# Second attention layer, edge stage: running sums kept in two PSUM accumulator banks and copied out by ScalarE at each item

## The reference

```
q, k, v = h @ W_qkv + b_qkv                      # 8 heads of 32
score   = sum_d(q[dst] * k[src]) * SCALE         # per edge and head
ex      = exp(score - max over the edges of dst)
attn    = ex / (sum of ex over the edges of dst)
h_new   = segment_sum(attn * v[src], dst) @ W_out + b_out
```

## Time and profile before

| what | value |
|---|---|
| median of 3 runs | 2125.84 us (2121.98 to 2130.7) |
| profiled execution, first to last instruction | 2134.3 us |
| whole span: TensorE busy | 1761.5 us |
| VectorE busy | 1539.6 us |
| GpSimd busy | 1160.5 us |
| ScalarE busy | 1070.3 us |
| edge stage of the second layer, first gather to last sum | 1243.6 to 1899.9 us |

### The profile page before, as it was taken

One profiled execution on the slowest core, in us unless ns is written; L12 is line 12 of the kernel. 1 busy time (PEld: TensorE's weight loads), 2 busy tenths in 40 slices (PEclk: granted clock), 3 DMA queues, 4 the chain that ended last, 5 costly groups with the idle time before them and its releaser, 6 DMA issues. The chain is left out here.

```text
span 2134.3 us, 41549 instructions
## 1 busy us (share of the span) xinstructions
PE 1761.5 (83%) x10388; PEld 1537.1 (72%) x10389; DVE 1539.6 (72%) x2788; ACT 1070.3 (50%) x2353; POOL 1160.5 (54%) x1169
## 2 busy tenths in 40 slices
PE   3699999999999989828973868888888888866278
PEld 3499999999999979728972756666666766645267
DVE  5388888888888845643545849899999898847622
ACT  1677777777777726403420145445455454316133
POOL 0376666666666601462443457777777777512112
PEclk7799999999999989758996989999999999867579
DMA  3443333333333312133323566666666666524310
GB/s 96 133 121 111 104 108 108 104 107 108 105 106 108 98 31 80 69 124 98 119 75 98 193 185 189 189 188 188 193 191 186 190 187 188 148 65 141 115 38 29
DMA packets 132538, 267.55 MB, mean 125 GB/s; under 512 B 24030, under 2 KB 75888, under 8 KB 132407
## 3 DMA queue, kind: packets, MB, share of 16 engines
q0 software_dynamic: 63456, 191.61, 30.7%
q1 hardware_dynamic: 68534, 73.21, 11.2%
q10 hardware_dynamic: 416, 1.18, 0.2%
HBM read 225.34 MB, written 42.50 MB: 125 GB/s over the span
## 5 line engine op out<-in xcount | busy, mean ns | idle before, releaser
L319 POOL DMA_INDIRECT e_rows<-h_table,e_idx x440 | 453.4, 1030 | 214.1 <-issue 106.3
L1740 POOL DMA_INDIRECT a_rows<-kv_table,a_idx x440 | 476.1, 1082 | 135.8 <-issue 128.9
L619 PE MATMUL e_w<-w2h,e_hidl 128*128 128x256 f32 x880 | 247.7, 304 | 2.9 <-DVE e_msg L704 2.9
L589 PE MATMUL e_agg<-e_msg,e_hot 128*128 128x256 f32 x880 | 246.1, 402 | 0.0
L1822 PE MATMUL a_q<-q,a_spread 128*128 x880 | 233.7, 407 | 6.5 <-ACT a_spread L1782 6.3
L620 PE MATMUL e_w<-w2l,e_hidh 128*128 128x256 f32 x880 | 226.4, 280 | 0.0
L1853 PE MATMUL a_agg<-a_rows,x 128*128 128x264 f32 x880 | 226.2, 402 | 0.0
L704 DVE TENSOR_TENSOR e_msg<-e_w,e_rows 128x1024 f32<-128x1024 f32 x110 | 134.7, 1224 | 93.4 <-PE e_w L623 93.4
L1775 ACT ACTIVATE a_apart<-iota_n,dst_rel 128x128 f32<-128x128 f32 x440 | 140.6, 391 | 112.9 <-PE a_agg L1853 112.8
L1822 PEld LDWEIGHTS a_q<-q,a_spread 128*128 128x128 f32 x880 | 166.2, 199 | 38.9 <-issue 12.8
L1853 PEld LDWEIGHTS a_agg<-a_rows,x 128*128 128x128 f32 x880 | 168.2, 200 | 24.7
(11 more groups left out here) (456 smaller groups left out, 4221.4 us busy)
## 6 DMA issues: line engine op xcount, KB each, us to landing
e_ea<-in_eaT SPq DMA_DIRECT2D x220, 64.0 KB
m_rows<-expert_rows SPq DMA_DIRECT2D x32, 272.0 KB, 2.7
e_rows<-h_table,e_idx POOLq DMA_INDIRECT x440
a_rows<-kv_table,a_idx POOLq DMA_INDIRECT x440, 3.7
q_ab<-expert_out SPq DMA_DIRECT2D x50, 128.0 KB, 3.3
kv_table<-q_kv SPq DMA_DIRECT2D x25, 256.0 KB, 2.2
u_stage<-in_m_w SPq DMA_DIRECT2D x16, 256.0 KB
x<-in_x SPq DMA_DIRECT2D x1, 3200.0 KB, 13.9
```

The costliest lines, as they stand in the source:

```text
L319: c.nc.gpsimd.indirect_dma_start(out=rows[:, g.slot8, j, :], out_offset=None, in_=table, in_offset=bass.IndirectOffsetOnAxis(ap=idx[:, g.s ...
L589: last = mm(bank(wins[j]), hot[:, g.slot4, t, :], msg[:, g.slot4, t, :], start=False, stop=False, skip_group_check=True)
L619: mm(w, hidl[:, g.slot, cols[k]], w2h[:, k, :], start=(k == 0), stop=False)
L1740: nc.gpsimd.indirect_dma_start(out=rows[:, g.slot * IG + j, 0:2 * D], out_offset=None, in_=c.kv_dram, in_offset=bass.IndirectOffsetOnAxis( ...
```

## The change

- The sums no longer go through SBUF for every group. Two banks hold the running sums of the current window and the one before or after it, chosen by the window's parity. `add_item` on TensorE opens the *other* bank with a two-column matmul of zeros and adds one item to its own bank. ScalarE's `keep` copies the bank over the window's place in `c.sums` after each item. TensorE waits for that copy before the next item.
- The sums are one step later: group i-7 in step i (`SUM = LAG + 1`). The first item stands between the two halves of the q matmuls of step i (after both in place 3 of a chunk), the second at the end of the step.
- In ScalarE's queue the first copy heads the step, the second follows the spread copy.
- VectorE's per-group addition is gone. The rescaling moves to the bank, one step later (place 3), and reads a ScalarE copy of the factor (`grown`).
- The one-hot ring grows from 10 to 12 groups. The memset of the sums in `project_qkv` is gone; the edge stage starts with a small memset and two ScalarE copies that clear the banks.

```diff
@@ project_qkv, GpSimd
-                nc.gpsimd.memset(c.sums[:, :, :], 0.0).then_inc(s_clr, 1)
-                pool.wait_ge(s_clr, 1)
@@ attention_edges
+    SUM = LAG + 1
+    HR = 12
...
+        bank = lambda w: ap[:, bass.ds(w & 1, 1), 0:DM].rearrange("p a d -> p (a d)")
+        other = lambda w: ap[:, bass.ds((w + 1) & 1, 1), 0:DM].rearrange("p a d -> p (a d)")
@@ GpSimd
+                nc.gpsimd.memset(zero[:, :], 0.0).then_inc(s_zero, 1)
-                        need(pool, c.sem("poolgate"), (s_idx, g.n + 1), (s_agg, g.n - R + 1))
+                        need(pool, c.sem("poolgate"), (s_idx, g.n + 1), (s_agg, (g.n - R + 1) * JG))
@@ ScalarE
+                act.wait_ge(s_zero, 1)
+                for p in range(2):
+                    nc.scalar.copy(ap[:, p, 0:DM], zero[:, :]).then_inc(s_zero, 1)
+                def keep(a, j, wins):
+                    need(act, s_ag, (s_agg, a.n * JG + j + 1))
+                    nc.scalar.copy(window(c.sums, wins[j]), bank(wins[j])).then_inc(s_acc, 1)
                 def step(at):
                     i = at(0)
+                    a = at(-SUM)
+                    if real(a):
+                        wins = item_windows(act, c, a.n)
+                        keep(a, 0, wins)
...
-                        need(act, s_ag, (s_agg, g.n - R + 1), (s_hot, g.n))
+                        need(act, s_ag, (s_agg, (g.n - HR + 1) * JG), (s_hot, g.n))
...
                         nc.scalar.copy(spread[:, h.pair, :, :].rearrange("p a n -> p (a n)"), hT[:, :]).then_inc(s_sp, 1)
+                    if i.place == 2 and closed(i.chunk - 1):
+                        need(act, s_ag, (s_gr, i.chunk), (s_rs, 2 * (i.chunk - 1)))
+                        nc.scalar.copy(grown[:, :], grow).then_inc(s_gn, 1)
+                    if real(a):
+                        keep(a, 1, wins)
@@ TensorE
+                def add_item(m, j, both):
+                    own = (both + j) >> 1
+                    need(pe, None, (s_msg, m.n + 1), (s_acc, m.n * JG + j), *([(s_rs, 2 * m.chunk + 2)] if m.place == 0 and j == 0 else []), own=True)
+                    mm(other(own)[:, 0:2], none[:, :], none[:, 0:2], start=True, stop=False, skip_group_check=True)
+                    for half in range(CT):
+                        t = j * CT + half
+                        last = mm(bank(own), hot[:, hots(m, t), :], rows[:, m.slot * IG + t, D:ROW], start=False, stop=False, skip_group_check=True)
+                    last.then_inc(s_agg, 1)
...
                         for j in range(IG):
+                            if j == CT and real(m) and not late:
+                                add_item(m, 0, sums)
...
                             last = mm(qp[g.pair][:, j * D:(j + 1) * D], spread[:, g.pair, j, :], window(c.q, wins[j // CT]), start=True, stop=True)
                         last.then_inc(s_q, 1)
+                        if real(m) and late:
+                            add_item(m, 0, sums)
...
                     if real(m):
-                        need(pe, None, (s_msg, m.n + 1), (s_acc, m.n), own=True)
-                        mm(ap[:, 1, 0:DM], none[:, 0:P], none[:, 0:DM], start=True, stop=False, skip_group_check=True)
-                        for j in range(JG):
-                            ...
+                        add_item(m, 1, sums)
@@ VectorE
-                    a = at(-LAG - 1)
-                    if real(a):
-                        w = ahead.take(i.step, "sums", a.n)
-                        need(dve, s_dg, (s_agg, a.n + 1), (s_acc, a.n), *([(s_rs, 2 * a.chunk + 2)] if a.place == 0 else []))
-                        to = c.sums[:, bass.ds(w, JG), :]
-                        v.tensor_tensor(to, to, ap[:, :, 0:DM], ALU.add).then_inc(s_acc, 1)
+                    if i.place == 3 and closed(ch):
+                        w = ahead.take(i.step, "crossing", ch * (CH // IG))
+                        need(dve, s_dg, (s_gn, ch + 1), (s_acc, (i.n - SUM) * JG))
+                        to = bank(w)[:, 0:D].rearrange("p (h d) -> p h d", h=H)
+                        v.scalar_tensor_tensor(to, grown[:, :].rearrange("p (h a) -> p h a", a=1).broadcast_to([P, H, DH]), 1.0, to, ALU.add, ALU.mult).then_inc(s_rs, 1)
...
```

More of the change, by code:

```diff
@@ L1776, in step @@
                         need(act, s_ag, (s_ap, (g.n + 1) * IG))
-                        nc.scalar.activation(hot[:, four(g), :], apart[:, :, :], ACT.Relu, bias=1.0, scale=-1.0).then_inc(s_hot, 1)
+                        nc.scalar.activation(hot[:, hots(g, 0):hots(g, IG), :], apart[:, :, :], ACT.Relu, bias=1.0, scale=-1.0).then_inc(s_hot, 1)
                     h = at(2)
@@ L1811, in step @@
                         mm(carries[:, 0:2 * (CH + 1)], c.heads_of_row[:, :], c.carried[:, :, :].rearrange("p a t -> p (a t)"), start=True, stop=True).then_inc(s_ca, 1)
+                    m = at(-SUM)
+                    sums = ahead.take(i.step, "sums", m.n) if real(m) else None
+                    late = i.place == 3
                     g = at(1)
+                    if real(m) and not real(g):
+                        add_item(m, 0, sums)
                     if real(g):
@@ L1826, in step @@
                         tr(exs, exT[:, :], c.ident[:, :]).then_inc(s_xT, 1)
-                    m = at(-LAG)
-                    if real(m):
-                        moved = ahead.take(i.step, "sums", m.n) & 1
                     if real(at(2)):
                         ahead.fetch(i.then, "q", at(2).n)
-                    if real(at(1 - LAG)):
-                        ahead.fetch(i.then, "sums", at(1 - LAG).n)
+                    if real(at(1 - SUM)):
+                        ahead.fetch(i.then, "sums", at(1 - SUM).n)
                     h = at(2)
@@ L1838, in step @@
                         for j in range(IG):
-                            last = tr(hT[:, j * P:(j + 1) * P], hot[:, h.slot * IG + j, :], c.ident[:, :])
+                            last = tr(hT[:, j * P:(j + 1) * P], hot[:, hots(h, j), :], c.ident[:, :])
                         last.then_inc(s_ht, 1)
@@ L1845, in step @@
                     if real(m):
-                        need(pe, None, (s_msg, m.n + 1), (s_acc, m.n), own=True)
-                        mm(ap[:, 1, 0:DM], none[:, 0:P], none[:, 0:DM], start=True, stop=False, skip_group_check=True)
-                        for j in range(JG):
-                            to = ap[:, 0, 0:DM] if j == 0 else ap[:, bass.ds(moved, 1), 0:DM].rearrange("p a d -> p (a d)")
-                            for half in range(CT):
-                                t = m.slot * IG + j * CT + half
-                                last = mm(to, hot[:, t, :], rows[:, t, D:ROW], start=(j == 0 and half == 0), stop=False, skip_group_check=True)
-                        last.then_inc(s_agg, 1)
+                        add_item(m, 1, sums)
                     if i.place == 0 and closed(ch):
@@ L1859, in _ @@
                 pe.wait_ge(s_none, 1)
+                pe.wait_ge(s_zero, 3)
                 rounds(pe, step, 4, LAG + 1, Edges)
@@ L1896, in step @@
                         v.tensor_tensor(by_head(rows[:, four(m), D:2 * D]), by_head(rows[:, four(m), D:2 * D]), ex, ALU.mult).then_inc(s_msg, 1)
-                        ahead.fetch(i.then, "sums", m.n)
-                    if i.place == 2 and closed(ch):
-                        w = ahead.take(i.step, "crossing", ch * (CH // IG))
-                        need(dve, s_dg, (s_gr, ch + 1), (s_acc, i.n - LAG))
-                        to = c.agg[:, bass.ds(w, 1), 0:D].rearrange("p a (h d) -> p (a h) d", h=H)
-                        v.scalar_tensor_tensor(to, grow.rearrange("p (h a) -> p h a", a=1).broadcast_to([P, H, DH]), 1.0, to, ALU.add, ALU.mult).then_inc(s_rs, 1)
-                        to = flat(c.agg[:, bass.ds(w, 1), D:DM])
-                        v.scalar_tensor_tensor(to, grow, 1.0, to, ALU.add, ALU.mult).then_inc(s_rs, 1)
                     if real(i):
```

24 lines of the change are left out of this document (16 added, 8 removed).

## The result

The changed kernel takes 2192.01 us (median of 4 runs, 2186.57 to 2194.59), the kernel before 2126.73 beside it (4 runs, 2121.98 to 2130.7). The ratio is 1.0304, 95% interval 1.0284 to 1.0323. The forecast was 2156 with a range to 2182: the slower direction and the circle of waits came true, the size did not, +65 us for +30.

What follows compares the result with a forecast made beforehand. GpSimd's unbroken gathers, 5.59 us a group, bound the kernel before; the change closes a longer circle of waits. + 33 - 6 + 0.6 + 2 = + 30 us, 2134.3 to 2164 profiled, 2156 us as median; 8-in-10 range 2120 to 2182.

Steps and rivals of the forecast that it cites:

- The removed addition is worth nothing: Edge stage: dropping VectorE's additions, 76.7 us in all, gives GpSimd nothing back; its 5.59 us a group stays.
- rival 2: Edge stage: GpSimd's long gathers go too, a group could fall to 5.0 us; 2062 us, or 2092 for half; chance 0.08.
- A plain step of 5.57: Edge stage: one full circle of copy, one-hots, spread, half of q and first item takes 5.57 us.
- Place 1's carries, + 0.2: Place 1 of a four-step chunk: the carries matmul stands ahead of q and waits for scans, + 0.2 us.
- Places 2 and 3, + 1.18: Per chunk: first item behind all q matmuls + 0.92, exponentials' copy ahead of spread + 0.16, rescaling + 0.1 us.
- it just fits; I take + 0.1: Place 3: VectorE's rescaling, 4.2 us, is done before the first item by TensorE's route, 4.5; + 0.1 us (0 to 0.5).
- the steps' + 33: Edge stage: about 25 chunks at 23.66 us against 22.36 now, + 33 us; bounds + 13 and + 56.
- The memset, - 6: End of the projection: without GpSimd's memset, VectorE's stalled normalisation comes back, - 6 us (-4.7 to -6.2).
- the start, + 0.6: Start of the edge stage: two clearing copies stand ahead of the first row numbers, + 0.6 us.
- The end, + 2: End of the edge stage: about seven rounds of 6.0 us against six of 6.31, + 2 us (-8 to + 6).
- 1: Edge stage: the circle is shorter than GpSimd's period, GpSimd stays the bound, only the ends change; 2122 us; chance 0.12.
- 3: Edge stage: TensorE's clock falls; with a quarter of the steps so, + 45 us on top, 2200 us; chance 0.10.

Runs made afterwards that it cites:

- e4: Kernel before with VectorE's msg (v times ex) cut from 1024 to 32 columns: 2059.81 us, ratio 0.9696 to before.
- e3: Kernel before with VectorE's addition into the sums cut from 264 to 8 columns an item: 2103.37 us, ratio 0.9891 to before.
- f2: Changed kernel with TensorE's tails matmul ahead of the second item instead of behind it: 2177.39 us, ratio 1.0229 to before.
- g3: Changed kernel with VectorE's product ahead of msg in place 2 alone: 2179.01 us, ratio 1.0244 to before.
- e1: Changed kernel with GpSimd's memset of the sums put back at the projection's end: 2198.89 us, ratio 1.0339 to before.
- f3: Changed kernel with two unread fill matmuls behind each item of the last eight steps: 2178.79 us, ratio 1.0242 to before.
- f1: Changed kernel with ScalarE's one-hots moved from ahead of the spread copy to the step's end: 2183.72 us, ratio 1.0275 to before.
- g2: Kernel before with the memset moved early and four unread matmuls behind each group's sums in the last seven steps: 2119.50 us, ratio 0.9973.
- g1: Kernel before with GpSimd's memset of the sums moved to the start of its block: 2122.69 us, ratio 0.9989 to before.

## Why the prediction fell short

- **GpSimd bounds the kernel before, through gathers lengthened by msg: right** (e4, expected 2060, measured 2059.81).
- **The removed addition is worth nothing: wrong as a statement on before** (e3, -19.5 us, of which 11 to 15 in the steps). The earlier trace rows does show that an addition lengthens no gather beside it; the step from there to "gives GpSimd nothing back" failed, since the addition sets when msg comes. It did no harm to the forecast's sum, since the changed stage is bound by another circle. But it means that rival 2's gain was partly real (mean gather 1.093 to 0.999) and that the new circle ate it. The rule of the Trainium skill (SBUF — State Buffer, "Who interferes with whom") was also quoted too narrowly: the section names VectorE's two-port modes as a second way to contend, and the memset's pair, where the normalisation reads one tensor, can only be a case of that one.
- **A plain step of 5.57: right** (5.54), by luck, as errors cancel: q to the two-column matmul 0.78 for 0.92, item's end to copy 0.36 for 0.43, and from the two-column matmul to the item's end 1.36 for 1.16, since the next matmul starts 0.22 us behind it and not 0.03 as in the earlier trace rows, with register work for the bank between. (The bounds of 5.45 and 5.65 don't follow from the links listed, which give 5.50 and 5.61; with these the sum is the same.)
- **Place 1's carries, + 0.2: too small, 0.50.** I priced the matmul and not what it stands behind. The chain begins a step earlier: the tails matmul waits behind the second item (1509.50), VectorE's three small instructions follow (1509.87 to 1510.48), carries at 1510.54, q at 1510.87. 0.30 x 25 chunks = 7.5 us; f2 takes the whole 0.50 away.
- **Places 2 and 3, + 1.18: too small, 1.50.** The step that failed was "it just fits; I take + 0.1". VectorE's work from msg to the end of the rescaling was priced right (1519.61 to 1523.74, 4.13 for 4.2). Two links beside it were left out: 0.42 from the start of the exponentials' copy to msg, and 0.47 from the rescaling to the two-column matmul, 5.02 in all. TensorE's own route takes 4.58 by g3 (1515.11 to 1519.69), for the 4.5 priced. So VectorE came last. With its hold gone the excess is 1.03 (g3), for 0.92 + 0.16: the term taken at 0.1 was 0.47, less 0.05 on the other two. 0.32 x 25 = 8 us.
- **Longer steps** that no median shows, 0.12 a chunk, 3 us; no run was spent on them. With these three, less 3 us for the plain step, the steps' + 33 becomes the measured + 49.
- **The memset, - 6: right within its range** (5.0 by the normalisations of all profiles; e1 alone shows 7), **and the start, + 0.6, too** (18.1 us from the last normalisation to the first q matmuls, 17.5 before). 
- **The end, + 2: the worst term, + 15.4.** This term failed by 13 us, more than any other. The clock was taken right and the links were not: from a copy's end to the two-column matmul 0.47 us, for 0.1 to 0.3; to the first record 0.22, left out; four records 2.11, item to copy 0.39, copy 0.38: 3.57 for 2.9 to 3.1. I also counted seven against six rounds of items; counted from the msg of group 102 it is eight on either side. The changed kernel's begin 6.0 us later behind the last q matmuls and take 7.4 each for 6.2 of before, the rounds with scans included: 6.0 + 8 x 1.18 = 15.4. f3 shows what the clock alone holds, 13 us; the links themselves are read from the timeline, and no run varied them.
- **Rivals.** 1 didn't happen, nor did 2 as a whole: the gathers got shorter, the stage did not. 3 did not either: the granted clock in the steps is 1.00, above the 0.97 of before, though the time was near that rival's 2200.

## What to carry to other kernels

When an operation moves to an engine that has time, draw the circle of waits through the in-order queues: a copy at the head of a queue makes everything behind it wait for the same item. Price each link from the wait's end to the next instruction's start, with its register work, and look for the next circle beneath, as f1 shows; here each was nearly as long as the period of before (5.54 and 5.23 for 5.59 us). And where a step has small instructions that once had slack (tails, rescaling), ask what they stand behind and not how long they are.

## What the runs showed of the hardware

- A VectorE multiplication of 1024 columns with both inputs in SBUF costs GpSimd's indirect gathers 0.14 us each in the mean (1.093 for 0.948). A gather that starts while it runs and is lengthened ends 0.81 to 0.83 us behind it, so what it loses depends on when it starts: single ones take up to 2.4 us for 0.95.
- An instruction that lengthens no gather can still be worth GpSimd's time, by its place in VectorE's queue: without the addition, which has one input in PSUM, the multiplication meets the gathers later in its run, and they take 1.056 us for 1.093 (e3).
- TensorE's granted clock at the end of the stage was 0.57, mostly the lower level of 1.2 GHz, with TensorE idle 1 us or more between items. With two more matmuls an item it was 1.00, and an item's four records fell from 2.11 to 1.15 us. That took 13 us off the changed kernel (f3). In the kernel before, four more matmuls a round took off 3 us (g2 against g1).
- GpSimd's memset of 5.8 us stretched one VectorE instruction of 0.40 us to 5.1 us, and to 5.3 us again when put back.
